# First feed-forward of an eight-layer chain rebuilt: setup products moved ahead of its barrier, softmax and gate folded, tail normalised on ScalarE

## What is computed

```python
query = h @ Wq.T                                        # 64 wide
router_scores = (query @ Wr.T) @ (aux_keys @ Wr.T).T / sqrt(48) + log_rel   # 128 slots
top_idx = top_k(router_scores, 8)
attn = query . aux_keys[top_idx] / sqrt(64) + log_rel[top_idx]
w = softmax(attn)                                       # over the 8 chosen
aux_out = (w @ aux_values[top_idx]) @ Wvd.T @ Wvu.T
var = jnp.var(h); log_var = log1p(var)
u = clip(log_var / (mean(log_var) + 1e-6) * 0.5 + sigmoid(gelu(h @ Wu1.T + bu1) @ Wu2.T + bu2) * 2.5, 0, 5)
gate = sigmoid(gate_w1 * clip((u - 0.5) / 1.5, 0, 1) + gate_bias);  gate = 0 where gate < 0.05
f(h) = h + gate * aux_out           # so the step gives layernorm(2 h + gate * aux_out)
```

## Time and profile before

| | before |
|---|---|
| median of 3 runs | 2022.72 us (2022.02 to 2025.67) |
| the profiled execution | 2025.79 us |
| its span, first to last instruction | 2024.1 us |
| busy share: TensorE, VectorE, ScalarE, GpSimd | 94%, 57%, 42%, 43% |
| mean granted TensorE clock | 0.977 |
| the feed-forward stage | about 261.7 to 323.9 us of the span |

### The profile page before, as it was taken

The page is one execution under the profiler, slowest core; times in us unless marked ns, Lnnn a source line. Parts: engine busy times, 40 slices in busy tenths (PEclk is TensorE's granted clock), DMA queues, the critical chain, the costliest instruction groups (busy, mean ns, idle before and its releaser), DMA issues.

```text
span 2024.1 us, 29824 instructions
## 1 busy us (share of the span) xinstructions
PE 1899.1 (94%) x11008; PEld 1289.1 (64%) x11008; DVE 1146.3 (57%) x2191; ACT 851.4 (42%) x1870; POOL 870.9 (43%) x1382
## 2 busy tenths in 40 slices
PE   6999967999999999999999799999999989999988
PEld 3544435888888888888887677774444454544456
DVE  5676456666666666666666432335455345566365
ACT  1565423444444444444444333314455502565441
POOL 2454306645454545454545344323344302443352
PEclk9999978999999999999999899999999999999999
DMA  6113000101010101010100134203122102111101
GB/s 214 39 35 107 1 11 1 53 1 53 1 53 1 53 1 53 1 53 1 53 1 32 45 128 141 98 0 96 49 64 85 54 0 74 39 34 43 50 10 42
DMA packets 46210, 94.60 MB, mean 47 GB/s; under 512 B 7689, under 2 KB 35721, under 8 KB 43145
## 3 DMA queue, kind: packets, MB, share of 16 engines
q1 hardware_dynamic: 43474, 90.34, 13.5%
q10 hardware_dynamic: 2592, 2.36, 0.5%
HBM read 61.68 MB, written 2.10 MB: 32 GB/s over the span
## 4 chain that ended last, share of the span: by engine, by line
PE 79%; DVE 11%; ACT 4%; issue 3%; DMA 1%; POOL 1%; POOLq 0%; SPq 0%; ACTq 0%; DVEq 0%
PE PS L1374 9%; PE PS L1455 9%; PE PS L458 6%; PE PS L561 6%; PE PS L539 5%; PE PS L1874 5%; PE PS L505 5%; PE PS L586 4%; PE PS L1433 4%; PE PS L1887 3%; PE PS L1385 3%; PE PS L1417 3%; PE PS L473 2%; PE PS L1845 2%; PE PS L507 2%
## 5 line engine op out<-in xcount | busy, mean ns | idle before, releaser
L971 ACT ACTIVATE PB<-PS 128x512 f32<-128x512 f32 x480 | 280.8, 599 | 237.2 <-PE PS L539 234.2
L878 POOL TENSOR_SCALAR_AFFINE_SELECT PB<-PB 128x256 f32<-128x256 f32 (+1 forms) x480 | 173.3, 365 | 320.3 <-ACT PB L971 314.0
L750 DVE TENSOR_REDUCE NM<-PS 128x2 f32<-128x1024 f32 x192 | 209.2, 1091 | 169.3 <-PE PS L507 167.9
L505 PE MATMUL PS<-KQ 96*128 96x512 bf16 (+3 forms) x768 | 186.4, 308 | 17.1 <-DVE NM L750 10.7
L539 PE MATMUL PS<-KQ 99*128 99x512 bf16 (+3 forms) x768 | 183.3, 304 | 4.8 <-ACT PB L971 3.4
L1772 POOL TENSOR_SCALAR PR<-PR,RCP 128x512 f32<-128x512 f32 (+3 forms) x256 | 134.6, 536 | 107.4 <-DVE RCP L1570 107.3
L1583 DVE TENSOR_REDUCE NX<-PS 128x1 f32<-128x512 f32 (+3 forms) x256 | 124.7, 488 | 77.6 <-PE PS L1406 71.9
L458 PE MATMUL PS<-XTT,WA 128*128 128x512 f32 x288 | 145.7, 612 | 13.4 <-DVE ident_masks_b L2501 12.0
L1641 ACT CAST OTH<-PS 128x512 fp32r<-128x512 f32 x64 | 37.5, 587 | 282.0 <-PE PS L1438 282.0
L507 PE MATMUL PS<-ident_masks_b 128*128 128x128 bf16 x768 | 149.7, 223 | 0.0
L1705 ACT ACTIVATE PR<-PS,NX 128x512 f32<-128x512 f32 (+3 forms) x256 | 136.8, 535 | 26.8 <-DVE NX L1583 22.8
(11 more groups left out here) (322 smaller groups left out, 4624.9 us busy)
## 6 DMA issues: line engine op xcount, KB each, us to landing
KQ<-HI SPq DMA_DIRECT2D x90, 128.0 KB, 2.4
KQ<-MID SPq DMA_DIRECT2D x72, 128.0 KB, 2.4
WB<-f_w SPq DMA_DIRECT2D x12, 768.0 KB, 4.4
WB<-w1o SPq DMA_DIRECT2D x8, 1024.0 KB, 7.9
WC<-f_w SPq DMA_DIRECT2D x10, 768.0 KB, 4.3
WB<-w1a SPq DMA_DIRECT2D x8, 768.0 KB, 4.4
WB<-w1b SPq DMA_DIRECT2D x8, 768.0 KB, 5.9
WA<-w SPq DMA_DIRECT2D x6, 1024.0 KB, 6.3
```

The costliest lines, as they stand in the source:

```text
L505: pe.matmul(ps, KQ[0:SR, self.query(G, h), i * P:(i + 1) * P], KQ[0:SR, self.key(G, h), 0:n], start=True, stop=False)
L750: x = dve.tensor_reduce(nm[:, h:h + 2, i], PS[:, b:b + 2, 0:(i + 1) * P], AX.X, ALU.max, negate=True)
L878: pool.affine_select(blocks, blocks, [[0, count], [1, P]], ALU.is_ge, 0.0, base=0, channel_multiplier=-1).then_inc(s16["probs_ready"].sem, 1)
L971: act.activation(PB[:, n % PBS, :], PS[:, 4 + n % 2, :], ACT.Exp, scale=self.scale)\
```

## The change

It does the following.

- `choose` reads the route products from PSUM. log_rel comes in by a 65th row: QF and G have 65 partitions, the last is ones in QF (`ones`) and log_rel in G. RS is gone, and with it the additions; the mask is made by one addition of minus TAKEN (now 1e30) fused with the attention scores; the negated maximum goes as the bias into four Exp of 128x128 that give the row sums as well (`accum_out`).
- Gate and reciprocal are no longer multiplied into the weights. They are one factor for a row (`weigh`, with 0.5), and the tail computes y * row + x, with epsilon divided by 4, instead of 2 x + y. The weights can be turned as soon as Exp is done.
- RK, AV, the query of batch 0, G and P are made by TensorE between the tiles of the first attention's last tail (`First16.follow`), and copied by ScalarE in its queue there.
- In the feed-forward's tail ScalarE makes the finish: `x = S * rstd + shift`, and GpSimd makes the column `shift = -mean * rstd` after each root.
- Batch 1 is chosen inside the tail, after the second mean; its Exp, its weights and their transposes follow in the other queues.
- One-column Sigmoid and Exp activations stand ahead of the places that need those tables.
- V of the next attention, and its projections 0 and 1 (high products first, low ones when XLa is ready), are issued in the feed-forward's stage; the low part of B1 too. In the attention, rope_low of projections 0 and 1 goes to VectorE, rope of projection 2 stands between the maxima of head 0, and XLb's low part is made after head 0.

```diff
@@ Tail
             def __init__(self, b, y_tile=None, y_done=None, mul=None, add=None, times=1.0,
-                         last=False, banks=False, biased=None, after=None):
+                         last=False, banks=False, biased=None, after=None, rows=None):
+                self.rows, self.eps = rows, EPS if rows is None else EPS / times ** 2
...
+                    if self.rows is not None:
+                        row = self.rows[:, NT * self.b + t:NT * self.b + t + 1]
+                        st.link(dve.scalar_tensor_tensor(src, y, row, self.XB[:, t, :], ALU.mult, ALU.add))
+                    else:
+                        st.link(dve.scalar_tensor_tensor(src, self.XB[:, t, :], self.times, y, ALU.mult, ALU.add))
...
+            def shift(self, pool, t):
+                pool.wait_ge(self.s_r.sem, self.s_r.at(t + 1))
+                pool.tensor_scalar(shift[:, t % 2, :], mv[:, t % 2, 0:1], rstd[:, t % 2, :], -1.0,
+                                   ALU.mult, ALU.mult).then_inc(s_shift.sem, 1)
+            def finish_scalar(self, act, u):
+                act.wait_ge(s_shift.sem, NT * self.b + u + 1)
+                act.activation(self.XB[:, u, :], S[:, u % 2, :], ACT.Identity, bias=shift[:, u % 2, :],
+                               scale=rstd[:, u % 2, :]).then_inc(self.s_x.sem, 1)
@@ Attention16, end of tensor and of scalar
-                self.tails[1].tensor(pe)
+                tail = self.tails[1]
+                for t in range(NT + 2):
+                    if t < NT:
+                        self.y_tile(pe, t, PS[:, t, :]).then_inc(tail.s_y.sem, 1)
+                    self.follow(pe, t)
+                    if t >= 2:
+                        if t >= 4:
+                            pe.wait_ge(tail.s_t.sem, tail.s_t.at(t - 3))
+                        tail.turn(pe, t - 2, PS[:, tail.t_bank(t - 2), :])
-                self.tails[1].scalar(act)
+                for t in range(NT):
+                    self.follow_scalar(act, t)
+                    self.tails[1].take(act, t, PS[:, self.tails[1].t_bank(t), :])
@@ Ffn0
+            def begin(self, pe, t):
+                if t == 1:
+                    ...  RK, AV into banks 6, 7
+                elif t == 3:
+                    pe.wait_ge(f0["rk_ready"].sem, 1)
+                    self.query(pe, 0)
+                    pe.wait_ge(f0["av_ready"].sem, 1)
+                    self.products(pe, PS[0:64, 7, 0:P], [(f0_Wr, RKT[:, :])], "g_psum")
+                elif t == 4:
+                    pe.wait_ge(f0["q_ready"].sem, 1)
+                    self.products(pe, PS[:, 6, :], [(AVT[:, :], f0_WvuT)], "p_psum")
...
             def tensor(self, pe):
+                pe.wait_ge(f0["g_ready"].sem, 3)
+                self.route(pe, 0)
+                pe.wait_ge(f0["p_ready"].sem, 1)
+                self.uncertain(pe, 0)
+                self.uncertain(pe, 1)
+                ...  sum of log variances
+                self.turn_weights(pe, 0)
+                pe.wait_ge(f0["gelu_ready"].sem, NB)
+                ...  sixteen one-column products
+                self.query(pe, 1)
                 pe.wait_ge(f0["wT_ready"].sem, 1)
                 for n in range(NB * NT + 2):
                     if n < NB * NT:
                         ...
+                        if n >= 2:
+                            before, u = self.tails[(n - 2) // NT], (n - 2) % NT
+                            pe.wait_ge(before.s_v.sem, before.s_v.at(u + 1))
                         self.y_tile(pe, b, t).then_inc(self.tails[b].s_y.sem, 1)
                     if n == 1:
-                        self.turn_weights(pe, 1)
+                        self.route(pe, 1)
+                    if n == 3:
+                        self.turn_weights(pe, 1)
+                    if n == 6:
+                        pe.wait_ge(self.tails[0].s_t.sem, self.tails[0].s_t.at(NT))
+                        a1.project_v(pe, 0, (0, 1))
+                    if n == 8:
+                        a1.project_v(pe, 0, (2, 3))
+                    if n in (8, 9):
+                        a1.begin_high(pe, n - 8)
                     if n >= 2:
                         ...  turn of tile n - 2
+                for p in (0, 1):
+                    a1.begin_low(pe, p)
@@ Ffn0.scalar
-                for b in range(NB): ... Gelu;  Exp(0); high a; high b; Exp(1);  Sigmoid, Sigmoid;  W0T copies
+                Ln;  a1.high(act, 0, "a");  a1.high(act, 0, "b");  self.exp(act, 0)
+                Gelu, Gelu;  one-column Sigmoid;  self.take_weights(act, 0);  self.ones(act, 1)
+                Sigmoid (learned);  Sigmoid (gate);  one-column Exp;  QF copy of batch 1
                 for b in range(NB):
                     for t in range(NT):
+                        n = NT * b + t
+                        if n == 0:
+                            self.tails[0].finish_scalar(act, 0)
+                            self.tails[0].finish_scalar(act, 1)
+                        elif n + 1 < NB * NT:
+                            self.tails[(n + 1) // NT].finish_scalar(act, (n + 1) % NT)
                         self.tails[b].take(act, t, self.x_bank(b, t))
+                        if b == 0 and t == 0:
+                            self.exp(act, 1)
+                            self.take_weights(act, 1)
                     if b == 0:
                         ...
                         a1.x_high(act, 0)
@@ Ffn0.gpsimd
+                a1.low(pool, 0, "b")
+                for t in range(NT):
+                    self.tails[0].root(pool, t)
+                    self.tails[0].shift(pool, t)
                 for t in range(NT):
                     self.tails[1].root(pool, t)
+                    self.tails[1].shift(pool, t)
+                    if t >= 1:
+                        a1.x_low(pool, 0, (t - 1,))
+                a1.x_low(pool, 0, (3,))
@@ Ffn0.choose
-                ... two additions of log_rel into RS
+                for t in range(NT):
+                    st.done(dve.max(M8[:, t, :], rps[:, t, 0, :]))
+                st.wait()
+                for t in range(NT):
+                    st.done(dve.match_replace(MRP[:, b, t, :], M8[:, t, :], rps[:, t, 0, :], TAKEN))
+                st.wait()
+                st.link(dve.scalar_tensor_tensor(MRP[:, b], MRP[:, b], -TAKEN, rps[:, :, 1, :], ALU.add, ALU.add))
+                dve.tensor_reduce(GA[:, 10, b * NT:(b + 1) * NT], MRP[:, b], AX.X, ALU.max, negate=True)
@@ Attention1
-                for p in (0, 1): self.project(pe, p)
-                self.project_v(pe, 0)
                 for _ in self.project(pe, 2):
...             # VectorE
                 self.rope(dve, 0)
                 self.rope(dve, 1)
+                self.rope_low(dve, 0)
                 self.take_v(dve, 0)
-                self.rope(dve, 2)
-                self.low_v(dve, 0)
+                self.rope_low(dve, 1)
...             # in head 0
+                        if n == 0 and i == 1:
+                            self.rope(dve, 2)
+                        if n == 0 and i == 2:
+                            self.low_v(dve, 0)
...             # GpSimd
-                self.low(pool, 0, "b")
                 for p in range(3):
                     self.sum(pool, p)
-                    self.rope_low(pool, p)
-                self.x_low(pool, 1)
...
+                    if n == 0:
+                        self.rope_low(pool, 2)
                     ... sum(ahead)
+                    if n == 0:
+                        self.x_low(pool, 1)
```

More of the change, by code:

```diff
@@ L1146, in __init__ @@
             def __init__(self):
-                one = Tail(0, self.y_tile, times=2.0)
-                self.tails = [one, Tail(1, self.y_tile, times=2.0, after=one)]
+                one = Tail(0, self.y_tile, times=2.0, rows=GA[:, 2, :])
+                self.tails = [one, Tail(1, self.y_tile, times=2.0, after=one, rows=GA[:, 2, :])]
             def y_tile(self, pe, b, t):
@@ new lines, in products, with query, uncertain @@
+            def products(self, pe, ps, pairs, s):
+                for i, (a, b) in enumerate(pairs):
+                    x = pe.matmul(ps, a, b, start=(i == 0), stop=(i == len(pairs) - 1))
+                x.then_inc(f0[s].sem, 1)
+            def query(self, pe, b):
+                self.products(pe, PS[0:64, 6 + b, :], [(f0_Wq[:, c, :], XTT[:, b, c, :]) for c in range(NC)], "q_psum")
+            def uncertain(self, pe, b):
+                self.products(pe, PS[:, 6 + b, :], [(f0_Wu1[:, c, :], XTT[:, b, c, :]) for c in range(NC)], "u_psum")
@@ new lines, in begin @@
+            def begin(self, pe, t):
+                if t == 1:
+                    pe.wait_ge(S_f0.sem, 16)
+                    self.products(pe, PS[0:48, 6, 0:P], [(f0_WrT, f0_keysT)], "rk_psum")
+                    self.products(pe, PS[0:32, 7, 0:P], [(f0_Wvd[:, c, :], f0_avT[:, c, :]) for c in range(NC)], "av_psum")
+                elif t == 3:
[6 more added lines that the diff above has]
```

(43 more changed lines are left out.)

172 lines of the change are left out of this document (69 added, 103 removed).

## The result

| | before | after |
|---|---|---|
| median of 4 runs each, same chip | 2022.51 us | 2007.77 us (2007.31 to 2011.87) |
| ratio, 95% interval | | 0.9928 (0.9911 to 0.9946) |
| the profiled execution, its span | 2025.79, 2024.1 | 2011.87, 2010.2 |
| granted clock, whole span | 0.977 | 0.981 |
| granted clock, 264 to 336 us | 0.81 | 0.84 |

What follows compares the result with a forecast made beforehand. TensorE bounds the long attention after the edited stage, so savings before about 360 us reach the end in full. Gain 18.5 us less 0.8 for the clock, 2022.7 - 17.7 = 2005.0 us; range 1998.5 to 2012.

Steps and rivals of the forecast that it cites:

- C: Mark: first score of the next attention's third head (head 2); forecast at 340.5 us, 18.5 us earlier.
- Part 1: Setup products moved ahead of the barrier, into the attention's last tail: that stage ends 1.9 us later.
- A: Mark: first residual sum of the feed-forward's tail; forecast at 282.4 us, 19.4 us earlier.
- Part 2: Head of the feed-forward's stage, from its start at 263.7 us to mark A at 282.4.
- rival (b): More is gained, 3 to 7 us; a combined ln and exp table set would save 1.3 us; chance 0.17.
- Part 3: Feed-forward's tail from A to the stage's end: 2.03 us a tile, barrier at 311.7 us where it was 323.9.
- Part 4: Start of the next attention: 8.0 us to B, then 10 us to head 1; C at 340.5 us.
- B: Mark: first score matmul of the next attention; forecast at 319.8 us, 18.5 us earlier.
- rival (d): GpSimd falls behind at heads 1 and 2 of the attention, its 1.5 us slack goes: 2 to 5 us lost; chance 0.10.
- I take 0.8 off for TensorE's clock: Allowance in the sum for TensorE at half clock in the edited stretch: 0.8 us off the 18.5 us gain.
- Rival (a): TensorE's clock at half in the new stage's idle stretches: 12 us at most, 4 to 12 gives 2009 to 2017; chance 0.15.
- (c): Slower than before: GpSimd's shift in the tail's two-slot loop would have to take 5.9 us, for 2027; chance 0.03.

Runs made afterwards that it cites:

- run 11: Changed kernel with the setup products back behind the barrier, plus filler products on TensorE that nobody reads: 2008.9 us, ratio 0.994.
- run 4: Changed kernel with the small setup products, query of batch 0, G and P back behind the barrier, without fillers: 2010.8 us, ratio 0.9958.
- run 5: The changed kernel itself, measured and profiled once more with nothing altered: 2007.36 us, ratio 0.9929; its profiled execution took 2003.8 us.
- run 8: Changed kernel plus products nobody reads in four places where TensorE waits (3, 6, 3 and 6): 2000.06 us, ratio 0.99.
- run 1: Changed kernel with the finish of the feed-forward's tail back on VectorE and no shift column, without fillers: 2007.29 us, ratio 0.9933.
- run 10: Changed kernel with the tail's finish back on VectorE, no shift column, plus fillers 3, 6, 3 and 6: 1997.88 us, ratio 0.9881.

## Why the prediction was right, and where it was off

- **What bounds, and that all arrives at the end.** Right: 98.40 us of 100 from 350 on, and C to the last score within 1.0 us.
- **Part 1, stage start 1.9 us later** (2.0 by its own marks, 261.7 and 263.7). Right: 2.2, measured from the common point. Undone, it costs 8.8 to 11.0 us with fillers (run 11) and 3.4 without (run 4, 2010.8 to 2007.4; the two medians are of different chips). The rest of A's advance, 11.7 of 15.6 us (run 4), stands with the setup undone, by one profile. It belongs to the folded choice and gate and the new order, which no run undid; how it divides among them is open.
- **Part 2, 18.7 us from the start to A.** It took 22.4. ScalarE's chain to the sixteen products took 12.4 us where 12.3 was forecast. In it the Exp's load stays behind Ln's (269.38, 1.28 us), so the combined set of the Trainium skill ("ScalarE: Activation LUTs", section "Table sets: the hidden batching unit") isn't used, and rival (b) loses that term. MAX8 and MATCH_REPLACE8 from PSUM cost 0.28 each as from SBUF. What failed is the price of products and query: 1.95 and 3.4 forecast, 3.2 and 5.6 measured, at a clock of 0.50; at full clock 1.95 and 3.65 (runs 5 and 8). At full clock the terms hold; what failed is that the clock was put in elsewhere and too small.
- **Part 3, 29.3 us from A to the barrier.** 29.2 came, but not for the reasons given. The shift took 0.26 us without a hop to speak of (0.45 taken), the root beside it 0.55 and no longer 0.75, ScalarE's pass 0.81 (0.8). With such prices the loop over two slots is as short as I had it, and still it isn't the loop that sets the tail but TensorE's queue. What failed is "With the finish left on VectorE the tile would be 2.31 rather than 2.03, eight tiles 2.2 us": the times of runs 1 and 10 show 0, and at full clock the tail shows 0.7 (run 10). That 29.2 us came out is in part luck: at full clock the stretch took 27.9 (runs 8 and 11). The rule that I weighed against it, VectorE for plain adds and multiplies (the Trainium skill, "ScalarE: Activation LUTs", section "Rules for kernel authors"), is borne out as to the price, 0.66 against 0.81, and neither loses nor wins time here that the medians show.
- **Part 4, 8.0 us from the barrier to B.** 7.5. VectorE's low part of k took 1.53 us and not 0.7 while GpSimd worked, and q's 0.54 when GpSimd was idle. The timeline shows both:

```profile
318.81 1.00 POOL L1850 TENSOR_TENSOR RA<-RA,RB 128x384 f32<-128x384 f32 x1
318.83 1.53 DVE L1626 TENSOR_TENSOR kL<-RA,kH 128x512 fp32r<-128x512 f32 x1 [0.52 <-ACT kH L1753]
...
320.96 0.54 DVE L1626 TENSOR_TENSOR qL<-RA,qH 128x384 fp32r<-128x384 f32 x1
321.55 0.50 PE L1507 MATMUL PS<-kH,qH 128*128 128x512 f32 x1 [0.63 <-DVE qL L1626]
331.10 0.80 PE L1507 MATMUL PS<-kH,qH 128*128 128x512 f32 x1 [4.24 <-POOL qL L1626]
```

- **Head 1 to head 2, 10.5 us.** 13.25 came, at 0.50 from 332 to 336. With the clock at 1.00 it is 10.6 (run 8). At head 2 no wait for GpSimd appears, so rival (d), GpSimd falling behind there, did not come; the wait of 4.24 us for it is at head 1 and lay within the 10 us that B to head 1 was given (9.6).
- **Sum and rivals.** The mis-sized term is "I take 0.8 off for TensorE's clock". In the profile it measured 7.2 us, 4.4 in the second execution. Other steps were 2 us too dear, so 5.1 us were missing at C, 2.8 in the median. That the time came so near is in part luck, since the two errors have opposite signs. Rival (a) named the mechanism, and its places were right only in part: it named 286 to 291 and 312 to 330. The low clock came at 276 to 282, on the query that it had priced but sooner than the places it named, and then at 294 to 298, 316 to 320 and 330 to 336, each time right behind a wait. The stage's end, 6.5 of the rival's 12 us, ran at 1.00. (c) is refuted by its own row: 0.26 us where 5.9 was needed.

## What to carry to other kernels

When a change shortens the waits around TensorE but leaves some, price the work right behind each remaining wait at half clock, not the wait itself; a few products that nobody reads, sized by their measured 0.67 us each, gave back 7 us here, and twice as many gave back nothing. How much of the 7 was won where they stand is open. Before a pass is moved to another engine for the sake of pace, look at what releases the busy engine in the new order: VectorE's tail waited for TensorE, so relieving VectorE won nothing that the times show. Take a mark ahead of the edits as zero when two profiles are compared, since two executions of one program differed here by 3 us at C.

## What the runs showed of the hardware

- The same program, profiled twice, has its first low clock of the stage at 276 to 282 us in one and within 264 to 274 us in the other. The two are 8.1 us apart in time (2011.87 and 2003.80), most of it behind the last score.
- GpSimd's power on one column took 0.55 us in the mean with the shift's TENSOR_SCALAR between two of them (the changed kernel) and 0.75 without it (run 1, where the first took 0.55 and the other seven 0.78 to 0.79). Why is open.
- A VectorE subtraction of two SBUF operands took 1.53 us beside a GpSimd addition, against 0.54 for three quarters of the width alone. By the width, 128x512 alone would take an estimated 0.7, so the extra is some 0.8 us; it started 0.02 us behind the GpSimd addition of 1.00 us and ended 0.55 us behind its end. With this the Trainium skill agrees ("SBUF — State Buffer", section "SBUF: two separate sides"): a VectorE instruction with two SBUF inputs and a GpSimd instruction that reads SBUF lock each other out for a whole instruction.
- ScalarE's Identity with a scale and a bias column took 0.81 us at 128x512, its Gelu with one column 0.69.
